# GpSimd adds one group's planes and TensorE starts its sums earlier in the closing of a macaron block

## What is computed

```python
x = x + 0.5 * ffn(layernorm(x))      # mixture of 16 experts, top 4 of each token
x = x + attention(layernorm(x))      # 16 heads of width 16
x = x + 0.5 * ffn(layernorm(x))      # the same experts again

def ffn(x):
    t = x * rsqrt(mean(x * x) + EPS) * norm_w
    vals, idx = top_k(t @ gate_w.T + gate_b, 4)
    G = zeros(M, 16); G[m, idx] = softmax(vals)
    h = einsum('mh,eoh->emo', t, w1) + b1
    act = min(h_even, 7) * sigmoid(1.702 * a) * (clip(h_odd, -7, 7) + 1)
    y = einsum('emi,edi->emd', act, w2) + b2
    return x + einsum('me,emd->md', G, y)
```

## Time and profile before

| | |
|---|---|
| median of 3 runs | 857.47 us |
| the three runs | 861.89, 857.47, 848.75 us |
| the profiled execution's own time | 850.03 us |
| its span in the trace | 848.3 us |
| granted TensorE clock, mean | 0.944 |
| VectorE busy | 584.2 us, 69% of the span |
| TensorE busy | 716.4 us, 84% |
| GpSimd busy | 401.6 us, 47% |

### The profile page before, as it was taken

The page is one execution under the profiler, slowest core; times in us unless marked ns, Lnnn a source line. Parts: engine busy times, 40 slices in busy tenths (PEclk is TensorE's granted clock), DMA queues, the critical chain, the costliest instruction groups (busy, mean ns, idle before and its releaser), DMA issues.

```text
span 848.3 us, 18026 instructions
## 1 busy us (share of the span) xinstructions
PE 716.4 (84%) x4747; PEld 566.9 (67%) x4747; DVE 584.2 (69%) x1375; ACT 439.5 (52%) x1066; POOL 401.6 (47%) x449
## 2 busy tenths in 40 slices
PE   2547537999999999879998898788669999999995
PEld 2534326778888887756776676556448888888883
DVE  3837427987777777557885785574757777777777
ACT  3644314665555555337674664444525555655551
POOL 5856750545555546432335431433633455554453
PEclk9999858999999999999997997888899999999999
DMA  7948658968986562464342232216656788787777
GB/s 308 373 169 305 232 215 315 316 230 278 326 268 218 186 211 84 146 226 175 145 160 102 106 128 90 95 39 216 216 173 217 234 277 250 254 267 232 234 253 267
DMA packets 77917, 181.02 MB, mean 213 GB/s; under 512 B 12016, under 2 KB 36864, under 8 KB 73856
## 3 DMA queue, kind: packets, MB, share of 16 engines
q1 hardware_dynamic: 38752, 95.03, 33.3%
q0 software_dynamic: 14928, 49.97, 15.4%
q10 hardware_dynamic: 24144, 34.88, 12.8%
HBM read 97.60 MB, written 65.45 MB: 192 GB/s over the span
## 4 chain that ended last, share of the span: by engine, by line
PE 40%; DVE 7%; issue 4%; another core or an unknown queue 3%; ACT 2%; ACTq 1%; POOL 1%; DVEq 0%; POOLq 0%
PE s_psT L1238 12%; PE s_psG L1265 6%; PE s_psO L1862 3%; PE s_psS L1827 3%; PE s_psG L1799 2%; PE s_psS L1186 2%; PE s_psS L1200 2%; DVE s_a_nm L2095 2%; PE s_psT L1843 2%; PE s_psT L1847 1%; PE s_psG L1812 1%; PE s_psG L1909 1%; POOL rows L1715 1%; PE s_psR L1934 1%
## 5 line engine op out<-in xcount | busy, mean ns | idle before, releaser
L1238 PE MATMUL f_bank<-weights,f_e_th 128*128 x316 | 120.4, 479 | 18.5 <-DVE f_e_hb L1314 10.1
L1481 POOL DMA_INDIRECT kbuf<-f_e_ys,f_e_place x79 | 81.5, 1031 | 113.5 <-ACT f_e_ys L1426 101.8
L1481 POOL DMA_INDIRECT kbuf<-s_e_own_ys,s_e_own_place x79 | 79.1, 1001 | 92.4 <-ACT s_e_own_ys L1426 79.9
L1238 PE MATMUL s_psT<-s_e_own_weights,s_e_own_th 128*128 x316 | 112.1, 455 | 7.4 <-ACT s_e_own_th L1451 3.8
L2095 DVE TENSOR_REDUCE s_a_nm<-s_psS 128x4 f32<-128x1024 f32 x64 | 78.3, 1223 | 55.8 <-PE s_psS L1827 42.0
L1715 POOL DMA_INDIRECT rows<-s_a_row,s_a_slot_i x64 | 62.9, 983 | 106.0 <-DVE s_a_slot_i L2222 86.6
L1238 PEld LDWEIGHTS f_bank<-weights,f_e_th 128*128 128x128 f32 x316 | 62.4, 198 | 40.4 <-issue 22.4
L1314 DVE TENSOR_TENSOR f_e_hb<-f_bank,f_e_bias 128x512 f32<-128x512 f32 x79 | 54.3, 687 | 50.9 <-PE f_bank L1238 32.4
L1314 DVE TENSOR_TENSOR s_e_own_hb<-s_psT,s_e_own_bias 128x512 f32<-128x512 f32 x79 | 54.3, 688 | 47.7 <-PE s_psT L1238 47.6
L2362 ACT ACTIVATE s_a_pT<-s_psT 128x1024 f32<-128x1024 f32 x62 | 63.3, 1022 | 43.0 <-PE s_psT L1847 31.1
L735 POOL DMA_INDIRECT rows<-f_r_row,f_r_slot_i x64 | 64.2, 1004 | 33.8 <-issue 19.7
(11 more groups left out here) (401 smaller groups left out, 1844.0 us busy)
## 6 DMA issues: line engine op xcount, KB each, us to landing
s_e_own_weights<-w_split SPq DMA_DIRECT2D x12, 1024.0 KB
s_e_tb<-rows ACTq DMA_DIRECT2D x80, 144.0 KB
w_split<-weights ACTq DMA_DIRECT2D x7, 1536.0 KB
f_e_tb<-rows ACTq DMA_DIRECT2D x62, 144.0 KB
s_a_qs<-s_a_qk SPq DMA_DIRECT2D x32, 256.0 KB, 2.4
weights<-w_raw SPq DMA_DIRECT2D x10, 768.0 KB, 14.8
w_split<-weights POOLq DMA_DIRECT2D x5, 1536.0 KB, 7.7
s_a_ks<-s_a_qk SPq DMA_DIRECT2D x30, 256.0 KB, 2.4
```

What stands on the lines that cost most here:

```text
L1238: last = pe.matmul(psH[j][:, :], left[:, p % 2, j, k * P:(k + 1) * P], first_of(h, k)[:, bass.ds(at, 1), :], start=n == 0, stop=n == len(p ...
L1481: pool.indirect_dma_start(out=kbuf[:, :], out_offset=bass.IndirectOffsetOnAxis(ap=place[:, i % KEPT:i % KEPT + 1], axis=0), in_=ys[:, n, : ...
```

## The change

One of VectorE's six groups, group 5, goes to GpSimd, and MINE falls from 6 to 5. GpSimd adds plane 0 of it before its put of tile 76, plane 1 before tile 77, plane 2 before tile 78 and plane 3 after it. A chain on one semaphore makes it wait for each add's end. `all_put` now stands behind these adds. SyncE's last-plane loads come in the order 6, 7, 0, 1, 5, 2, 3, 4, and SyncE stores group 5 before group 4, after a wait for GpSimd's four adds. VectorE's plane 0 is now two adds in the first half and three in the second. TensorE does the first two of its group 6's matmuls (x and plane 0) in the drain, after the `result` of pair 37, and waits for each plane ahead of its matmul and no longer for all three ahead of the first one.

```diff
@@ experts, tensor @@
             if pair(s - 3):
                 for j in range(2):
                     result(s - 3, j)
+            if not first_layer and s == NP:
+                split.begin_sums(pe)
@@ experts, gpsimd @@
             if pair(s - 4):
                 put(2 * (s - 4) + 1)
+            if not first_layer and s in (NP + 1, NP + 2):
+                split.pool_sum(pool, 2 * (s - NP - 1))
             if pair(s - 3):
                 put(2 * (s - 3))
-        if not first_layer:
-            all_put(pool, s_add)
+            if not first_layer and s == NP + 1:
+                split.pool_sum(pool, 1)
@@ combine @@
-    MINE = NG - BY_PE
+    MINE = NG - BY_PE - 1
+    ours = lambda i: MINE + 1 + i
...
-            plane(k, range(MINE, NG) if k == TOP - 1 else range(NG))
-            if k == TOP - 1:
-                plane(k, range(MINE))
+            if k < TOP - 1:
+                plane(k, range(NG))
+            else:
+                plane(k, range(MINE + 1, NG))
+                plane(k, (0, 1, MINE))
+                plane(k, range(2, MINE))
         for g in range(MINE):
+            if g == MINE - 1:
+                sp.wait_ge(s_pd, TOP)
+                store(sp, MINE)
             sp.wait_ge(s_d, g + 1)
             store(sp, g)
...
+    def begin_sums(pe):
+        pe.wait_ge(s_in[0], 16 * NG)
+        pe.matmul(summed[0][:, :], c["ident"][:, :], xs[ours(0)], start=True, stop=False)
+        pe.matmul(summed[0][:, :], c["ident"][:, :], planes[0][ours(0)], start=False, stop=False)
+    split.begin_sums = begin_sums
...
+    def pool_sum(pool, k):
+        if k == 0:
+            pooled.append(Chain(pool, s_pd))
+        if k < TOP - 1:
+            pool.wait_ge(s_in[k], 16 * NG)
+        else:
+            pool.wait_ge(s_last[MINE], 16)
+        pooled[0].link(pool.tensor_tensor(xs[MINE], xs[MINE], planes[k][MINE], ALU.add))
+    split.pool_sum = pool_sum
+
+    @program.add("gpsimd")
+    def _(pool):
+        pool_sum(pool, TOP - 1)
+        all_put(pool, s_add)
...
     @program.add("tensor")
     def _(pe):
         ident = c["ident"][:, :]
-        for k in range(TOP - 1):
-            pe.wait_ge(s_in[k], 16 * NG)
         for i in range(BY_PE):
-            pe.matmul(summed[i][:, :], ident, xs[MINE + i], start=True, stop=False)
+            if i > 0:
+                pe.matmul(summed[i][:, :], ident, xs[ours(i)], start=True, stop=False)
             for k in range(TOP - 1):
-                pe.matmul(summed[i][:, :], ident, planes[k][MINE + i], start=False, stop=False)
-            pe.wait_ge(s_last[MINE + i], 16)
-            pe.matmul(summed[i][:, :], ident, planes[TOP - 1][MINE + i], start=False, stop=True).then_inc(s_sum, 1)
+                if (i, k) != (0, 0):
+                    pe.wait_ge(s_in[k], 16 * NG)
+                    pe.matmul(summed[i][:, :], ident, planes[k][ours(i)], start=False, stop=False)
+            pe.wait_ge(s_last[ours(i)], 16)
+            pe.matmul(summed[i][:, :], ident, planes[TOP - 1][ours(i)], start=False, stop=True).then_inc(s_sum, 1)
```

More of the change, by code:

```diff
@@ L2514, in combine @@
     s_in, s_last, s_d, s_out = [m.sem(f"in{k}") for k in range(TOP - 1)], [m.sem(f"last{g}") for g in range(NG)], m.sem("d"), m.sem("out")
-    s_vd, s_carrys, s_sum, s_kept = m.sem("vd"), m.sem("carrys"), m.sem("sum"), m.sem("kept")
+    s_vd, s_carrys, s_sum, s_kept, s_pd = m.sem("vd"), m.sem("carrys"), m.sem("sum"), m.sem("kept"), m.sem("pd")
     xs = [x[:, g * GPT:(g + 1) * GPT, :].rearrange("p t d -> p (t d)") for g in range(NG)]
     BY_PE = len(summed)
-    MINE = NG - BY_PE
+    MINE = NG - BY_PE - 1
+    ours = lambda i: MINE + 1 + i
     def store(queue, g):
@@ L2568, in _ @@
                 dve.tensor_tensor(xs[g - 1], xs[g - 1], planes[TOP - 1][g - 1], ALU.add).then_inc(s_d, 1)
+    def begin_sums(pe):
[3 more added lines that the diff above has]
+    split.begin_sums = begin_sums
+    pooled = []
+    def pool_sum(pool, k):
[11 more added lines that the diff above has]
+        all_put(pool, s_add)
     @program.add("tensor")
@@ L2585, in _ @@
             act.wait_ge(s_sum, i + 1)
-            act.activation(xs[MINE + i], summed[i][:, :], ACT.Copy).then_inc(s_kept, 1)
+            act.activation(xs[ours(i)], summed[i][:, :], ACT.Copy).then_inc(s_kept, 1)
             act.wait_ge(s_kept, i + 1)
-            store(act, MINE + i)
+            store(act, ours(i))
 def second(program, nc, m, c, x, xn, table, rows, kbuf, proj, w_raw, w_split, b_first, out):
```

## The result

Over 20 runs each, the changed kernel's median is 855.5 us (851.5 to 864.26) and the one before's 853.34 (847.77 to 861.89). The ratio, made from fast runs alone, is 1.0059 with a 95% interval of 1.0033 to 1.0086: 5.0 us slower, between 2.8 and 7.3. Over all 20 runs the medians lie only 2.2 us apart and the means 3.8. By the 2% of this measurement that is "same". But the interval excludes zero: it is a loss of a few us, of which the closing alone shows 2.8.

What follows compares the result with a forecast made beforehand. VectorE's adds in the closing were taken as the bound: 3.7 us of holds by GpSimd less 2.4 saved gave +1.3, added to a four-execution mean of 854.5 for 856 us, range 847 to 864.

Steps and rivals of the forecast that it cites:

- The bound: Closing: VectorE's queue of adds sets SyncE's last store at 843.23 us; the 5.1 us behind it are fixed.
- Rival A: Closing: VectorE's and GpSimd's adds do not hold each other; GpSimd becomes last, -1.9 us; chance 0.22.
- Part 1: VectorE, closing: loses four adds of 0.60 us, saving 2.4 us, all on the path.
- Part 2: GpSimd, closing: gains four adds of 1.28 us, 5.1 in all; later puts are delayed, but no plane loads come later.
- add 0: GpSimd's plane 0 add behind the put of tile 75: 830.95 to 832.2 us, holding VectorE 0.46 us.
- Part 3: Closing: GpSimd's adds hold VectorE's by 0.46 + 3 x 1.09 = 3.7 us; less 2.4 saved, net +1.3 us.
- Add 1 waits for the turn: GpSimd's plane 1 add, after tile 76's put, waits for VectorE, runs 834.5 to 835.7 us and holds it 1.09.
- The upper bound: Closing: each GpSimd add holds VectorE its full 1.28 us; 5.1 - 2.4 = +2.7 us.
- Part 4: TensorE, drain and end: two matmuls moved earlier send ScalarE's last store 1.7 us earlier; cost nothing, gain nothing.
- Part 5: SyncE's order: group 5's load fifth, group 4's last, each there over 1 us before its add; costs nothing.
- B: Closing: GpSimd loses the turn to VectorE and ends last; +4.2 us, or +1.6 with less left over; chance 0.1.
- C: Closing: holds equal what is saved, part falling into waits for loads; 0 us within 0.5; chance 0.13.

Runs made afterwards that it cites:

- e1: Kernel before plus TensorE's part alone, no GpSimd adds: ratio 1.0037 (1.0000 to 1.0075) to before; last store starts 17.27 us after GpSimd's last clip, span end 21.75.
- e3: Changed kernel with GpSimd's four adds replaced by semaphore raises, group 5 stored without its planes: ratio 1.0010 to before; last store 15.06 us after the clip.
- e7: Kernel before with TensorE's part and VectorE's plane 0 and 1 adds moved into loop and drain: ratio 0.9998 to before; last store 14.87 us after the clip.
- e2: Kernel before plus GpSimd's part alone (group 5, changed load and store order), TensorE as before: last store 20.42 us after the clip, span end 25.1.
- e9: The changed kernel again, unchanged, on chip 8: ratio 1.0025 (1.0003 to 1.0047) to before; last store 20.41 us after the clip.
- e8: Changed kernel with all four GpSimd adds behind its last put: last store 19.76 us after the clip, span end 24.5.
- e10: Changed kernel with a one-element memset between each GpSimd put and its add: last store 19.34 us after the clip, span end 24.0.
- e5: Changed kernel with two one-operand clips in place of each GpSimd add: last store 18.09 us after the clip, span end 22.8.
- e4: Changed kernel with three memsets of group 5 in place of each GpSimd add: last store 17.74 us after the clip, span end 22.2.
- e13: TensorE's part alone again, against the kernel before on chip 0: ratio 0.9993 (0.9977 to 1.0009); last store 17.26 us after the clip.
- e0: Kernel before, unchanged, run again: SyncE's last store 17.27 us after GpSimd's last clip, span end 22.2.
- e11: Kernel before with one unused semaphore added: ratio 0.9992 (0.9972 to 1.0012) to before on chip 8; last store 17.26 us after the clip.

## Why the prediction was wrong

**The bound** was read rightly as to VectorE's queue, with a wrong step behind it: "I take what is behind it (5.1 us) as fixed". It was 5.1 before, 4.7 after, 4.5 in e1, 6.7 in e3 and 6.3 in e7. The stores' transfers share the DMA engines, and when they start closer together they land later. Rival A's -1.9 us for the case of no holds was wrong for that reason. e3, the nearest to that case, measured -0.6 us.

**Part 1**, 2.4 us saved on VectorE: right (e3: 2.4 to 2.5).

**Part 2**, GpSimd's adds of 1.28 us behind the put of tile 75, no plane later: right. (After the change the last plane's loads went out 0.8 us later after the clip than in the profile before, but in e2 and e9, with the same adds, at 4.6 and 4.2 us, earlier than before's 5.3.) The put of tile 75 grew from 0.96 to 1.49 beside VectorE's plane 0 adds, which come 0.6 earlier now; so add 0 began 5.3 us after the clip and not 5.0.

**Part 3** decided the sign, as it said, and the sign of the sum was right; its size is the step that failed. "Sum of the holds: 0.46 + 3 x 1.09 = 3.7 us" measured 0.90 + 1.52 + 1.51 + 1.40 = 5.3. The first was longer mainly because add 0 ended 0.3 us later than forecast. As to the others, the estimate of 1.09 from the clip holds where an add of GpSimd's is not directly behind a put (1.07 in e8 and e10). "Add 1 waits for the turn" is what didn't happen: behind a put it waited for nothing, and VectorE lost 0.3 to 0.45 us more each time. The clip from which I took the turns stands directly behind a put itself, and it waited; a two-operand add in that place does not, and no row of before could show that. The upper bound, 1.28 each, was too low for the same reason. It supposed that no hold is longer than GpSimd's add itself. The net was +2.9 on VectorE's end, where I had +1.3 and at most +2.7.

The rule that I quoted (the Trainium skill, "SBUF — State Buffer", "Who interferes with whom") stood up in kind in three runs: reads of one or two operands held VectorE (e5, e2), memsets didn't (e4), and VectorE's step with one SBUF operand wasn't held. That who comes first keeps the port for its whole instruction agrees with e8's three adds behind another add and with e10's of 771.87, which waited for the running add. The adds behind a put do not: VectorE's record begins first and VectorE is held all the same.

**Part 4**, TensorE's part at nothing: it gains 0.5 us alone (e1 and e13, span end 21.75 and 21.8), and nothing beside GpSimd's part (e2 and after both end at 25.1). "That is not the last to end: gain nothing", said of ScalarE's last store, was true of the one trace that I had; in e0 and e11 that store is the last to land.

**Part 5**, SyncE's order at nothing: 0.3 us lost. "Behind it is queued only the store of group 4" was true, but GpSimd's store itself, ready 5 us before, sits between those of groups 3 and 4 and its issue takes the time that group 4 then waits.

**Rivals.** B named a loss of 1.6 to 4.2 with GpSimd last; the +3.1 of the last store lies between, but GpSimd was done 5.4 us before VectorE. It never lost its turn. C (0 us) fell with the +2.9 on VectorE's end: e3 shows 2.5 saved, and the holds were 5.3.

**The number.** The forecast of 856 us is 0.5 from the median of 855.5, and that is no merit. It was a mean of four executions plus 1.3, and stood below the median of 857.47 that I had before me, so it read as a gain of 1.5 where the sum said a loss of 1.3. This is the second step that failed: "so I take the mean of all four" changed the starting point and with it the direction of the forecast. Over 20 runs before is 853.34, and the change measured 5.0 us against it (2.8 to 7.3) in the result and 2.0 (0.2 to 3.7) on chip 8.

## What to carry to other kernels

An elementwise instruction moved from VectorE to GpSimd is not hidden if VectorE meanwhile runs instructions with two operands in SBUF: count GpSimd's length less 0.2 us against VectorE (1.07 for an add of 1.27 here, 0.41 for a clip of 0.61), and 0.3 to 0.45 more for an add directly behind a scatter. An add of 0.60 us that takes 1.27 there then costs more than it saves. VectorE's steps that read PSUM were not slowed here, so such work belongs beside them, or beside VectorE's waits. And before an engine's last stage is shortened, look at what moves behind it: here, by the estimate above, the output's transfers left about 1 us of room, whatever the adds took.

## What the runs showed of the hardware that was not expected

- A 128x512 float32 add of GpSimd's directly behind an indirect DMA of its own held a running add of VectorE's for 1.37 to 1.52 us; behind another add or a one-element memset it held the next one for 1.07 to 1.08. A one-operand clip of 0.61 us held the next for up to 0.42, and waited for the running one, behind an indirect DMA too.
- VectorE's held add always ended 0.54 to 0.56 us after GpSimd's instruction, whether its own record began up to 0.37 before that instruction's or up to 0.5 after it.
- Three memsets of 0.53 us in each place held VectorE not at all.
- GpSimd's indirect DMA beside VectorE's two-operand adds took 0.97 to 1.50 us, once 2.24 (e4), without holding them.
- The stores of 256 KB landed 2.0 to 5.8 us after their issue, the longest while the last plane's loads were on their way; a single late one took 2.0.
- The same kernel took 854 us on one chip (granted TensorE clock 0.94 to 0.95) and 784.5 to 785.4 us on three others (0.97 to 0.98), with the closing the same to 0.1 us in SyncE's last store and the span's end.
